# Mixture-of-experts stages with weigh-and-add from the accumulators, in a Trainium2 kernel of two attentions and two expert stages

## The chip, the core and the metric

The kernel runs on one core of a Trainium2 chip. The core has five engines that run side by side: TensorE (PE in the profile, with its weight loads as PEld), VectorE (DVE), ScalarE (ACT), GpSimd (POOL) and SyncE (SP), which only issues transfers. They wait for each other through semaphores. Matmul results land in the accumulator memory (PSUM), eight banks of 512 fp32 columns by 128 partitions; everything else that is worked on lies in SBUF. The metric is device microseconds for one execution, as a median of several.

## What is computed

An input `x` of 4 x 512 tokens by 128 features goes through four stages, each of the form x + stage(layernorm(x)): an attention with two steps of test-time training of its inner weights, a mixture of experts, a block-causal attention with 16 heads, and the same mixture of experts again with the same weights. The mixture of experts is what the change touches:

```
x_flat = x.reshape(-1, d)                                   # 2048 tokens, d = 128
gates = softmax(x_flat @ Wg + bg)                           # 8 experts
topk_gates, topk_idx = top_k(gates, 2)
topk_gates = topk_gates / sum(topk_gates)
expert_out = einsum('nd,edo->neo', x_flat, We) + be         # all 8 experts, 128 outputs each
out = sum over the two chosen experts of expert_out * topk_gates
x = x + out
```

All eight experts are computed for every token, and each result is weighed with a weight `wt` that is zero for the six experts that weren't chosen.

## The kernel before

The tokens stand as 16 tiles of 128 (`NT` = 16), in four groups of four tiles (`BATCH`, `TPB`, `SEQ` = 512). The kernel runs as phases: `qkv_phase`, twice `gradient_phase` and `schulz_phase`, `query_phase`, then `moe_phase(0)`, `attention_phase` and `moe_phase(1)`. Within a phase each engine has an instruction list of its own, and `pipeline` (line 77) writes a software pipeline for an engine: each step has a lag in tiles, and the middle of it is a hardware loop over two tiles at a time. The order on an engine is what the list says; semaphores `s_...` tie the engines together.

fp32 products are made of two fp32r parts: a high part (`xh`) and the remainder (`xl`), and `mm3` (line 114) issues three matmuls, high by high, high by low and low by high, with its lines 117, 118 and 119 in the profile.

`moe_phase` (line 969) has two parts. **Logits and weights:** VectorE normalizes four tiles (`norm`, line 1143), TensorE transposes them into `psT` (line 1096), ScalarE copies the 512 columns to `xTs` (line 1047), GpSimd copies them again into `xnT` (line 1021), TensorE multiplies with `wg` in plain fp32 (line 1103, output of 8 partitions), ScalarE takes the result with the gate's bias added (line 1052), TensorE transposes it back in pieces of 8 x 128 (line 1109), VectorE takes it (line 1153). After the four groups VectorE runs a chain of small steps, each waiting for the one before it: softmax with ScalarE's exponential (line 1070), the best and the second-best expert (`best`, line 1168), and the weights `wt` (line 1183). TensorE transposes `wt` (line 1115), ScalarE and VectorE part it (lines 1076, 1192), and TensorE makes the biases of all tiles, four banks by three matmuls (line 1119), which VectorE adds to `x` (line 1197).

**Experts, tile by tile:** ScalarE makes `xh` (line 1061), GpSimd `xl` (line 1034), TensorE two banks of 512 columns with three matmuls each (line 1131, shown as lines 117 to 119, output `m_E_`). VectorE weighs experts 0 to 3 in one operation (`weigh`, line 1204), ScalarE experts 4 to 7 one by one (line 1083), both into `y`. Then the eight are added: GpSimd adds halves of 512 columns (`add_half`, line 1030), VectorE quarters of 256 (line 1212), eighths of 128 (line 1217), and the last sum to `x` (line 1222). In the first of the two stages VectorE also takes the layernorm statistics of the tile (line 176, `stats`). There are two pairs of banks for `m_E_` and two buffers for each of `y`, `z`, `z2`, `z3`.

The weights of these stages are loaded and parted long before: `load_later_weights` (line 585) issues the loads, `part_later_weights` (line 606) parts them on GpSimd in the second `schulz_phase`, before GpSimd's line 671.

Of the kernel before, what the change touches and what calls it, by code (L numbers as in the profile page):

```python
# [22 lines left out]
F32 = mybir.dt.float32  # L23
# [6 lines left out]
P = 128  # L30
# [91 lines left out]
class Kernel:  # L122
    def __init__(self, nc, ctx, args, out):
# [13 lines left out]
        self.wg, self.bg = sb("wg", [P, NE]), sb("bg", [NE, 1])  # L137
# [447 lines left out]
    def load_later_weights(self, sp):  # L585
# [7 lines left out]
            (self.bg[:, :], self.a["L0_ffn_bg"].rearrange("(n a) -> n a", a=1)),  # L593
# [12 lines left out]
    def part_later_weights(self, pool):  # L606
# [362 lines left out]
    def moe_phase(self, nth):  # L969
# [8 lines left out]
        s_xn, s_xT, s_xTs, s_keep, s_L, s_l = (sem(n) for n in ("xn", "xT", "xTs", "keep", "L", "l"))  # L978
        s_sh, s_e, s_c, s_wT, s_wTs, s_B, s_xb = (sem(n) for n in ("sh", "e", "c", "wT", "wTs", "B", "xb"))
        s_hi, s_lo, s_E, s_y, s_z, s_z2, s_z3, s_x, s_out = (sem(n) for n in ("hi", "lo", "E", "y", "z", "z2", "z3", "x", "out"))  # L980
        s_prio, s_w, s_lT, s_lTs = sem("prio"), sem("w"), sem("lT"), sem("lTs")
        ACT_E = 4
        with ExitStack() as c:
            sb = lambda n, s, d=F32: c.enter_context(nc.sbuf_tensor(f"m{nth}_{n}_", s, d))
            ps = lambda n, s, d=F32: c.enter_context(nc.psum_tensor(f"m{nth}_{n}_", s, d))
            weh, wel, wg, bg, beh, bel = self.weh, self.wel, self.wg, self.bg, self.beh, self.bel
            xn, xTs, xnT = sb("xn", [P, 2, TPB, P]), sb("xTs", [P, 2, SEQ]), sb("xnT", [P, TOK])
# [3 lines left out]
            lTs = sb("lTs", [NE, 2, SEQ])  # L991
            wTh, wTl = sb("wTh", [P, P], F32R), sb("wTl", [P, P], F32R)
            xh, xl = sb("xh", [P, 2, P], F32R), sb("xl", [P, 2, P], F32R)
            y, z, z2, z3 = sb("y", [P, 2, NE * P]), sb("z", [P, 2, 4 * P]), sb("z2", [P, 2, 2 * P]), sb("z3", [P, 2, P])
            psT, psL = ps("T", [P, 2, 512]), ps("L", [P, 2, 512])
            psE = ps("E", [P, 2, NE * P])
            block = c.enter_context(nc.Block())
            tile = lambda t: bass.ds(t.i * 2 + t.j, 1)
            FIRST = [Tile(0, j) for j in range(2)]
            later = lambda step: lambda t: None if t.number() in (0, 1) else step(t)  # L1000

            @block.sync
            def _(sp):
                if nth == 1:
                    dst = self.out.rearrange("b (t p) d -> p (b t) d", p=P)
                    for g in range(BATCH):
                        sp.wait_ge(s_x, (g + 1) * TPB + 2)
# [4 lines left out]
            def _(pool):  # L1012
# [642 lines left out]
```

## Time and profile before

| | us |
|---|---|
| median of 3 runs | 913.87 (912.15 to 914.26) |
| the profiled execution, own time | 913.51 |
| its span, first to last instruction | 911.7 |
| TensorE busy | 778.6 (85%) |
| VectorE busy | 600.5 (66%) |
| ScalarE busy | 420.7 (46%) |
| GpSimd busy | 376.6 (41%) |
| mean granted TensorE clock | 0.946 of 2.4 GHz |
| first mixture-of-experts stage | about 406 to 476 |
| second mixture-of-experts stage | about 842.6 to the end |

Busy time is from an instruction's start to its end as recorded, also where it stands still in between; on an engine one may start before the one ahead of it has ended, so the distance between starts can be shorter than a duration. The granted clock is 1.00 at 2.4 GHz and 0.50 at 1.2 GHz. All times of rows are microseconds from the start of the span, unless marked ns.

### The profile page before, as it was taken

What the parts mean: (1) busy time and instruction counts of PE and PEld (TensorE: products, weight loads), DVE (VectorE), ACT (ScalarE), POOL (GpSimd) and SP (SyncE); (2) the same over time, 40 slices, a digit from 0 to 9 for tenths busy, and PEclk for the clock granted to TensorE, in tenths of its full rate; (3) what the DMA queues carried; (4) which work ended last, traced back from release to release, by engine and by line L of the source; (5) the groups of instructions that cost most, each with busy time, mean ns of one, the idle gap of its engine ahead of it and who ended that gap; (6) DMA issues with size and microseconds to landing.
All of it is one profiled execution on the core that took longest, in us unless ns stands there. A gap on an engine that the chain in (4) does not pass through costs nothing. (4 is left out here: it accounts for less than half of the span.)

```text
span 911.7 us, 16940 instructions
## 1 busy us (share of the span) xinstructions
PE 778.6 (85%) x5464; PEld 594.6 (65%) x5464; DVE 600.5 (66%) x1621; ACT 420.7 (46%) x1190; POOL 376.6 (41%) x512
## 2 busy tenths in 40 slices
PE   3669999879999667968628999999999999998763
PEld 1249999758999656755315766777777777777442
DVE  3936665355655556766996767766676666664698
ACT  4743332433333223314534666565556555562453
POOL 4854443015445534204642443343334333332275
PEclk9979999989999978997987999999999999999798
DMA  3030000000000000000000000000000000000001
GB/s 99 1 128 1 0 0 1 1 0 1 1 0 0 1 0 1 1 1 0 0 0 1 2 1 2 2 1 2 2 1 1 2 1 1 2 1 2 1 12 35
DMA packets 9327, 7.00 MB, mean 8 GB/s; under 512 B 1456, under 2 KB 8880, under 8 KB 9136
## 3 DMA queue, kind: packets, MB, share of 16 engines
q1 hardware_dynamic: 9264, 6.18, 2.1%
q8 instruction: 37, 0.61, 0.3%
q14 instruction: 26, 0.21, 0.1%
HBM read 5.13 MB, written 1.05 MB: 7 GB/s over the span
## 5 line engine op out<-in xcount | busy, mean ns | idle before, releaser
L1356 POOL TENSOR_SCALAR t_p_<-t_p_,t_rinv_ 128x128 f32<-128x128 f32 (+3 forms) x256 | 132.5, 535 | 213.5 <-DVE t_rinv_ L1551 213.5
L1544 DVE CUSTOM_DVE_ANT_0 t_p_<-t_S_,t_mask_ 128x128 f32<-128x128 f32 (+3 forms) x256 | 112.8, 487 | 72.7 <-PE t_S_ L1443 69.2
L1386 ACT ACTIVATE t_p_<-t_p_,t_nmin_ 128x128 f32<-128x128 f32 (+3 forms) x256 | 140.0, 551 | 9.0 <-DVE t_nmin_ L1544 9.0
L1391 ACT ACTIVATE t_pT_<-t_T_ 128x384 f32<-128x384 f32 (+1 forms) x96 | 50.7, 528 | 128.3 <-PE t_T_ L1455 128.3
L1455 PEld LDWEIGHTS t_T_<-ident,t_p_ 128*128 128x128 f32 x640 | 68.3, 140 | 44.6 <-POOL t_p_ L1356 28.7
L1443 PE MATMUL t_S_<-t_k_,t_q_ 64*128 64x256 f32 (+3 forms) x512 | 95.0, 469 | 0.0
L1470 PE MATMUL t_O_<-t_pT_,t_v_ 128*64 128x128 f32 x1280 | 91.0, 280 | 0.1
L1455 PE MATMUL t_T_<-ident,t_p_ 128*128 128x128 f32 x640 | 91.0, 281 | 0.0
L1470 PEld LDWEIGHTS t_O_<-t_pT_,t_v_ 128*64 128x64 f32 x1280 | 67.9, 136 | 29.9 <-ACT t_pT_ L1391 26.5
L432 POOL TENSOR_TENSOR g_sp<-g_s,g_t 128x512 f32<-128x512 f32 x32 | 40.9, 1277 | 103.3 <-DVE g_t L553 103.3
L1555 DVE COPY t_pT_<-t_T_ 128x384 f32<-128x384 f32 (+1 forms) x96 | 57.3, 597 | 3.1 <-PE t_T_ L1455 3.0
L544 DVE TENSOR_TENSOR g_sw<-g_G,g_s 128x512 f32<-128x512 f32 x32 | 22.1, 692 | 55.3 <-ACT g_s L456 55.3
L1030 POOL TENSOR_TENSOR m_z_<-m_y_ 128x512 f32<-128x512 f32 x32 | 43.4, 1355 | 27.9 <-DVE m_y_ L1204 27.9
L117 PE MATMUL m_E_<-weh,m_xh_ 128*128 128x512 f32 x64 | 29.2, 456 | 29.5 <-issue 14.9
L1443 PEld LDWEIGHTS t_S_<-t_k_,t_q_ 64*128 64x128 f32 x512 | 41.3, 185 | 18.9 <-issue 15.8
L1386 ACT ACTIVATION_READ_ACCUMULATOR t_p_<-t_p_,t_nmin_ 128x1 f32 x256 | 48.7, 190 | 0.0
L465 ACT ACTIVATE g_hT<-g_H 128x512 f32<-128x512 f32 x32 | 19.1, 597 | 58.3 <-PE g_H L497 58.3
L438 POOL TENSOR_TENSOR g_w<-g_u,g_sp 128x512 f32<-128x512 f32 x32 | 41.3, 1292 | 3.6 <-POOL g_sp L432 2.2
L1217 DVE TENSOR_TENSOR m_z_<-m_z_ 128x128 f32<-128x128 f32 x32 | 39.6, 1238 | 0.8 <-DVE x L1222 0.5
L117 PEld LDWEIGHTS m_E_<-weh,m_xh_ 128*128 128x128 f32 x64 | 13.0, 204 | 41.3 <-POOL m_xl_ L1034 19.9
L1083 ACT ACTIVATE m_y_<-m_E_,m_wt_ 128x128 f32<-128x128 f32 x128 | 36.4, 368 | 6.0 <-PE m_E_ L119 6.0
L504 PEld LDWEIGHTS g_PT<-proj,g_hT 128*128 128x128 f32 x256 | 33.6, 192 | 2.6
(270 smaller groups left out, 1849.4 us busy)
## 6 DMA issues: line engine op xcount, KB each, us to landing
wqkv<-in_L_attn_b_w_qkv_dram SPq DMA_DIRECT2D x1, 1536.0 KB
x<-in_L_attn_a_x_dram SPq DMA_DIRECT2D x4, 256.0 KB, 4.0
out_dram<-x SPq DMA_DIRECT2D x4, 256.0 KB, 2.3
we<-in_L_ffn_We_dram SPq DMA_DIRECT2D x1, 512.0 KB
wout<-in_L_attn_b_w_out_dram SPq DMA_DIRECT2D x1, 512.0 KB
proj<-n_L_attn_a_ttt_proj_dram SPq DMA_DIRECT2D x1, 256.0 KB, 6.1
gv<-n_L_attn_a_ttt_gate_dram SPq DMA_DIRECT2D x1, 256.0 KB, 5.1
gv<-in_L_attn_a_ttt_val_dram SPq DMA_DIRECT2D x1, 256.0 KB, 5.7
```

Of the source, the lines that this page charges most:

```text
L117: e.matmul(out, ah, bh, start=start, stop=False)
L432: pool.tensor_tensor(sp_[:, t.ring, :], s_[:, t.ring, :], t1[:, t.ring, :], ALU.subtract).then_inc(g["sp"], 1)
L438: pool.tensor_tensor(w1[:, t.ring, :], u_[:, t.ring, :], sp_[:, t.ring, :], ALU.mult).then_inc(g["w1"], 1)
L1030: pool.tensor_tensor(z[:, t.ring, :], y[:, t.ring, 0:4 * P], y[:, t.ring, 4 * P:8 * P], ALU.add).then_inc(s_z, 1)
L1356: last = pool.tensor_scalar(pr[:, G.par, h, cols], pr[:, G.par, h, cols], rinv[:, G.par, n:n + 1], 1.0, ALU.mult, ALU.mult)
L1386: act.activation(pr[:, G.par, h, cols], pr[:, G.par, h, cols], ACT.Exp, bias=nmin[:, G.par, n:n + 1], scale=-1.0, accum_out=rsum[:, G.par, ...
L1391: act.activation(pT[:, G.par, 0, G.blocks], psT[:, 0, 0:G.width], ACT.Copy).then_inc(t["eA"], 1)
L1443: last = pe.matmul(psS[:, (2 * G.n + h) % 3, at_:at_ + (qt + 1) * P], qp[d, G.par, qt * P:qt * P + P], kp[d, G.par, 0:(qt + 1) * P], start ...
L1455: last = pe.transpose(psT[:, h, k:k + P], pr[:, G.par, h, at_:at_ + P], ident[:, :])
L1470: last = pe.matmul(psO[d, qt * P:qt * P + P], v[:, G.b % 2, n, G.p * P + h * DH:G.p * P + h * DH + DH], pT[:, G.par, h, at_:at_ + P], star ...
L1544: dve.tensor_tensor_reduce(pr[:, G.par, h, cols], psS[:, (2 * G.n + h) % 3, at_:at_ + keys], mask[:, SEQ - keys:SEQ], 1.0, -NEG, ALU.add, ...
L1555: dve.tensor_copy(pT[:, G.par, 1, G.blocks], psT[:, 1, 0:G.width]).then_inc(t["eB"], 1)
```

## The change

Both mixture-of-experts stages are rewritten; the attentions are left as they are.

- The normalized and transposed tiles are parted straight from the bank: ScalarE writes `xh`, VectorE `xl`, for all 2048 tokens, once. Logits are `mm3` products with `xh` and `xl` of a tile as the stationary operand and the parted gate weights (`wgh`, `wgl`, 8 columns) as the moving one; they land with tokens on partitions. The gate's bias is added on VectorE. The softmax's division is left out, since the two chosen weights are divided by their sum anyway.
- TensorE makes tiles 0 and 1, then the biases, then the other tiles. The banks are a ring of four pairs. Tiles 2 and 3 use the four banks of the biases and wait until VectorE has added them.
- VectorE no longer weighs into `y`. It does five steps per tile (`take`): bank times weight plus running sum, for experts 0, 2 into `a` (beginning with `x`) and 1, 3, 4 into `b` (beginning with `z`). The steps of one turn belong to two tiles, in the order 1, 0, 3, 2, 4, so that each depends on the one two before it.
- ScalarE weighs experts 5 to 7 into `y`; GpSimd adds these three to `z` in two operations, and closes each tile with x = a + b.
- The loops are written out, with no hardware loop.

```diff
-        self.wg, self.bg = sb("wg", [P, NE]), sb("bg", [NE, 1])
+        self.wg, self.bg = sb("wg", [P, NE]), sb("bg", [P, 1, NE])
+        self.wgh, self.wgl = sb("wgh", [P, NE], F32R), sb("wgl", [P, NE], F32R)
...
+        c(pool.tensor_tensor(self.wgh[:, :], self.wg[:, :], self.ones[:, 0:NE], ALU.mult))
+        c(pool.tensor_tensor(self.wgl[:, :], self.wg[:, :], self.wgh[:, :].bitcast(F32), ALU.subtract))
...
+            def experts_of(t, first, count=1):
+                at = (4, 6, 0, 2)[t % 4] + first * P // 512
+                return psAll[:, at, first * P % 512:first * P % 512 + count * P]
+
+            def sums(t, e):
+                turn = t + LATER[e]
+                here = [k for k in ORDER if 0 <= turn - LATER[k] < NT]
+                return (ON_DVE * turn - 3 if turn else 0) + here.index(e) + 1
...
-                def add_half(t):
-                    pool.wait_ge(s_y, t.done() + 2)
-                    pool.wait_ge(s_w, t.done() + 2)
-                    pool.wait_ge(s_z2, t.done())
-                    pool.tensor_tensor(z[:, t.ring, :], y[:, t.ring, 0:4 * P], y[:, t.ring, 4 * P:8 * P], ALU.add).then_inc(s_z, 1)
+                def close(t):
+                    pool.wait_ge(s_a, sums(t, 4))
+                    pool.tensor_tensor(x[:, t, :], a[:, t % 4, :], b[:, t % 4, :], ALU.add).then_inc(s_x, 1)
+
+                for t in range(NT):
+                    r = t % 4
+                    if t > 1:
+                        close(t - 2)
+                    pool.wait_ge(s_y, t + 1)
+                    if t > 3:
+                        pool.wait_ge(s_a, sums(t - 4, 1))
+                    pool.tensor_tensor(z[:, r, :], y[:, r, 0:P], y[:, r, P:2 * P], ALU.add).then_inc(s_z, 1)
+                    pool.wait_ge(s_z, 2 * t + 1)
+                    pool.tensor_tensor(z[:, r, :], z[:, r, :], y[:, r, 2 * P:3 * P], ALU.add).then_inc(s_z, 1)
...
+                for g in range(BATCH):
+                    act.wait_ge(s_xT, g + 1)
+                    act.activation(xh[:, block_of(g)], psT[:, g % 2, :], ACT.Copy).then_inc(s_xh, 1)
...
+                def logits(g):
+                    pe.wait_ge(s_xl, g + 1)
+                    for t in range(g * TPB, (g + 1) * TPB):
+                        last = mm3(pe, psL[:, 0, t * NE:t * NE + NE], xh[:, tile_of(t)], xl[:, tile_of(t)], wgh[:, :], wgl[:, :])
...
                 def experts(t):
-                    pe.wait_ge(s_lo, t.done())
-                    pe.wait_ge(s_y, t.done())
-                    pe.wait_ge(s_w, t.done())
+                    if t > 3:
+                        pe.wait_ge(s_y, t - 3)
+                        pe.wait_ge(s_a, sums(t - 4, 4))
+                    elif t > 1:
+                        pe.wait_ge(s_xb, BATCH)
...
+                def low(g):
+                    dve.wait_ge(s_xh, g + 1)
+                    dve.tensor_tensor(xl[:, block_of(g)], psT[:, g % 2, :], xh[:, block_of(g)].bitcast(F32),
+                                      ALU.subtract).then_inc(s_xl, 1)
...
-                g(dve.tensor_reduce(tot[:, :], gate[:, :, :], AX.X, ALU.add))
-                g(dve.reciprocal(rtot[:, :], tot[:, :]))
-                g(dve.tensor_tensor(gate[:, :, :], gate[:, :, :], wide(rtot), ALU.mult))
...
+                for n, bank in enumerate(banks):
+                    rows = x[:, n * TPB:(n + 1) * TPB, :].rearrange("p t d -> p (t d)")
+                    dve.wait_ge(s_B, n + 1)
+                    dve.tensor_tensor(rows, bank, rows, ALU.add).then_inc(s_xb, 1)
...
+                def take(t, e):
+                    if e == 0:
+                        dve.wait_ge(s_E, t + 1)
+                        dve.wait_ge(s_xb, t // TPB + 1)
+                        if t > 3:
+                            dve.wait_ge(s_x, t - 3)
+                    if e == 1:
+                        dve.wait_ge(s_z, 2 * t + 2)
+                    if e > 1:
+                        dve.wait_ge(s_a, sums(t, (0, 1, 3)[e - 2]))
+                    acc = (a, b)[LATER[e]][:, t % 4, :]
+                    so_far = (x[:, t, :], z[:, t % 4, :])[e] if e < 2 else acc
+                    dve.scalar_tensor_tensor(acc, experts_of(t, e), weight(t, e), so_far, ALU.mult, ALU.add).then_inc(s_a, 1)
+
+                for t in range(NT + 1):
+                    for e in ORDER:
+                        if 0 <= t - LATER[e] < NT:
+                            take(t - LATER[e], e)
+                    if nth == 0 and t > 3:
+                        stats(t - 4)
```

## Rows read from the trace of the kernel before

**Rows 1.** Stretches: us, busy (x count) of PE, PEld, DVE, ACT, POOL, clock, DMA share.

```profile
872.00:900.00 28.00, 17.24 (x65) 10.91 (x63) 28.00 (x42) 14.06 (x52) 19.46 (x22) 1.00 0.06 19
```

**Rows 2.** Timeline of the second stage's loop: start, us, engine, line, what, [idle before].

```profile
884.33 1.40 POOL L1030 TENSOR_TENSOR m_z_<-m_y_ 128x512 f32<-128x512 f32 x1 [0.83 <-DVE m_y_ L1204]
884.35 0.47 PE L117 MATMUL m_E_<-weh,m_xh_ 128*128 128x512 f32 x1 [1.07 <-POOL m_xl_ L1034]
884.50 1.38 DVE L1217 TENSOR_TENSOR m_z_<-m_z_ 128x128 f32<-128x128 f32 x1
886.27 0.68 DVE L1204 TENSOR_TENSOR m_y_<-m_E_,m_wt_ 128x512 f32<-128x512 f32 x1
...
900.54 0.47 PE L117 MATMUL m_E_<-weh,m_xh_ 128*128 128x512 f32 x1 [1.07 <-POOL m_xl_ L1034]
```

**Rows 3.** Timeline of VectorE: weights and end, first stage; end, second stage.

```profile
426.69 0.29 DVE L1183 TENSOR_TENSOR m_wt_<-m_sel_,m_rtot_ 128x128 f32<-128x128 f32 x1
...
474.82 0.48 DVE L176 BATCH_NORM_STATS2 stats<-x 128x6 f32<-128x128 f32 x2
...
908.51 0.49 DVE L1222 TENSOR_TENSOR x<-x,m_z_ 128x128 f32<-128x128 f32 x2
```

**Rows 4.** Timeline around the bias matmuls, second stage.

```profile
863.17 0.29 DVE L1183 TENSOR_TENSOR m_wt_<-m_sel_,m_rtot_ 128x128 f32<-128x128 f32 x1
...
864.69 0.50 PE L117 MATMUL m_T_<-beh,m_wTh_ 128*128 128x512 f32 x1 [0.76 <-DVE m_wTl_ L1192]
...
865.26 0.40 PE L119 MATMUL m_T_<-beh,m_wTl_ 128*128 128x512 f32 x1
...
867.36 0.40 PE L119 MATMUL m_T_<-beh,m_wTl_ 128*128 128x512 f32 x1
...
867.57 1.28 POOL L1030 TENSOR_TENSOR m_z_<-m_y_ 128x512 f32<-128x512 f32 x1
...
867.80 0.69 DVE L1197 TENSOR_TENSOR x<-m_T_,x 128x512 f32<-128x512 f32 x1 [1.96 <-PE m_T_ L119]
```

**Rows 5.** Groups by line and shape: what xcount | busy us, mean ns | idle before.

```profile
L839 DVE SCALAR_TENSOR_TENSOR gv<-acc,n_rate,gv 128x512 f32<-128x512 f32 x4 | 3.0, 751 | 3.1 <-PE acc L738 2.9
...
L822 DVE COPY n_A<-n_small 128x128 f32<-128x128 f32 x18 | 5.0, 280 | 0.0
...
L800 DVE TENSOR_SCALAR n_A<-n_small,n_r 128x128 f32<-128x128 f32 x12 | 3.8, 348 | 15.7 <-PE n_small L678 15.6
...
L1034 POOL TENSOR_TENSOR m_xl_<-m_xnT_,m_xh_ 128x128 fp32r<-128x128 f32 x32 | 15.5, 488 | 20.4 <-ACT m_xh_ L1061 20.4
...
L438 POOL TENSOR_TENSOR g_w<-g_u,g_sp 128x512 f32<-128x512 f32 x32 | 41.3, 1292 | 3.6 <-POOL g_sp L432 2.2
```

**Rows 6.** Timeline of VectorE, end of the first stage's loop.

```profile
467.13 0.28 DVE L1222 TENSOR_TENSOR x<-x,m_z_ 128x128 f32 x1
467.33 0.28 DVE L176 BATCH_NORM_STATS2 stats<-x  x1
```

**Rows 7.** Timeline of the second stage's logits.

```profile
847.17 0.60 ACT L1047 ACTIVATE m_xTs_<-m_T_ 128x512 f32<-128x512 f32 x1 [3.05 <-PE m_T_ L1096]
...
851.51 0.32 PEld L1109 LDWEIGHTS m_E_<-ident,m_lTs_ 8*128 8x128 f32 x4 [0.86 <-ACT m_lTs_ L1052]
...
855.97 0.19 DVE L1153 COPY m_logit_<-m_E_ 128x32 f32<-128x32 f32 x1 [0.65 <-PE m_E_ L1109]
...
856.52 0.29 DVE L1161 TENSOR_TENSOR m_logit_<-m_logit_,m_m_ 128x128 f32<-128x128 f32 x1
...
857.20 0.29 ACT L1070 ACTIVATE m_gate_<-m_logit_ 128x128 f32<-128x128 f32 x1
```

**Rows 8.** Stretches of one us before and at the bias matmuls.

```profile
857.00:858.00 1.00, 0.27 (x1) 0.30 (x2) 0.44 (x2) 0.49 (x3) 0.83 (x2) 0.50 0.00 0
...
864.00:865.00 1.00, 0.31 (x1) 0.30 (x2) 0.65 (x2) 0.96 (x4) 0.21 (x1) 1.00 0.00 0
```

**Rows 9.** Timeline of GpSimd in the second Schulz phase.

```profile
352.66 2.49 POOL L671 TENSOR_TENSOR gvl<-gv,gvh 128x512 fp32r<-128x512 f32 x2 [24.92 <-ACT gvh L776]
```

More of the change, by code:

```diff
@@ L1078, in weigh_last @@
-                def weigh_last(t):
-                    act.wait_ge(s_E, t.done() + 2)
-                    act.wait_ge(s_z, t.done())
-                    for n in range(NE - ACT_E, NE):
-                        cols = slice(n * P, n * P + P)
-                        last = act.activation(y[:, t.ring, cols], psE[:, t.ring, cols], ACT.Copy,
-                                              scale=wt[:, tile(t), n:n + 1].rearrange("p a e -> p (a e)"))
-                    last.then_inc(s_w, 1)
-                pipeline(act, (0, later(high)), (1, weights_high), (2, weigh_last))()
+                act.wait_ge(s_wT, 1)
@@ new lines, in _ @@
+                act.activation(wTh[:, :], psT[:, 0, 0:P], ACT.Copy).then_inc(s_wh, 1)
+                for t in range(NT):
+                    act.wait_ge(s_E, t + 1)
+                    if t > 3:
+                        act.wait_ge(s_z, 2 * t - 6)
+                    for k in range(NE - ON_DVE):
+                        e = ON_DVE + k
+                        last = act.activation(y[:, t % 4, tile_of(k)], experts_of(t, e), ACT.Copy, scale=weight(t, e))
+                    last.then_inc(s_y, 1)
@@ L1089, in _, with turn @@
             @block.tensor
             def _(pe):
-                def turn(t):
-                    pe.wait_ge(s_xn, t.done())
-                    if t.number() not in (0, 1):
-                        pe.wait_ge(s_xTs, t.done(-1))
+                def turn(g):
+                    pe.wait_ge(s_xn, g + 1)
+                    if g > 1:
+                        pe.wait_ge(s_xl, g - 1)
                     for n in range(TPB):
-                        last = pe.transpose(psT[:, t.ring, n * P:n * P + P], xn[:, t.ring, n, :], ident[:, :])
+                        last = pe.transpose(psT[:, g % 2, tile_of(n)], xn[:, g % 2, n, :], ident[:, :])
@@ L1097, in turn @@
                     last.then_inc(s_xT, 1)
                 def logits(g):
-                    pe.wait_ge(s_xTs, g.done())
-                    pe.wait_ge(s_lTs, g.done())
-                    pe.matmul(psL[0:NE, g.ring, :], wg[:, :], xTs[:, g.ring, :], start=True, stop=True).then_inc(s_lT, 1)
-                def turn_logits(g):
-                    pe.wait_ge(s_lTs, g.done() + 2)
-                    pe.wait_ge(s_l, g.done())
-                    for n in range(TPB):
-                        last = pe.transpose(psE[:, g.ring, n * NE:n * NE + NE], lTs[:, g.ring, n * P:n * P + P], ident[0:NE, 0:NE])
-                    last.then_inc(s_L, 1)
@@ L1136, in _ @@
+                turn(0)
+                for g in range(BATCH):
+                    if g + 1 < BATCH:
+                        turn(g + 1)
+                    logits(g)
+                experts(0)
+                experts(1)
+                biases()
+                for t in range(2, NT):
+                    experts(t)
             @block.vector
             def _(dve):
-                n = self.ln_vector(dve, s_var, s_root, s_ln)
-                dve.sem_inc(s_xT, 2)
-                dve.sem_inc(s_l, 2)
@@ L1219, in add_x @@
-                def add_x(t):
-                    dve.wait_ge(s_z3, t.done() + 2)
-                    dve.wait_ge(s_xb, 1)
-                    dve.tensor_tensor(x[:, tile(t), :], x[:, tile(t), :], z3[:, t.ring, :], ALU.add).then_inc(s_x, 1)
-                def stats(t):
-                    dve.wait_ge(s_x, t.done() + 2)
-                    self.take_stats(dve, t.i * 2 + t.j)
-                last = ((6, stats),) if nth == 0 else ()
-                pipeline(dve, (2, weigh), (1, add_bias), (3, add_quarter), (4, add_eighth), (5, add_x), *last)()
+                dve.wait_ge(s_wh, 1)
@@ L1231, in moe_phase @@
+                for t in range(NT + 1):
[4 more added lines that the diff above has]
+                        stats(t - 4)
+                if nth == 0:
+                    for t in range(NT - 3, NT):
+                        stats(t)
         if nth == 0:
```

185 lines of the change are left out of this document (62 added, 123 removed).

## The prediction

> **What bounds the kernel now.** The page comes first: no engine is busy throughout, and 85% for TensorE is a mean over stages. So I read the two mixture-of-experts stages by themselves. In a stretch of the second one's loop the table of stretches has VectorE busy all the time at 28.00 of 28 us, TensorE 17.24, GpSimd 19.46, ScalarE 14.06 [rows 1]. But VectorE's busy time is not work: in the timeline of one tile its 128x128 add of line 1217 takes 1.38 us, beginning as GpSimd's 1.40 us add of line 1030 runs and ending with it, where an operation of its shape elsewhere takes 0.28 [rows 2, 6]. It stands still beside GpSimd. The circle is: VectorE weighs (0.68), GpSimd adds the half (1.40), VectorE's next adds come free only then, VectorE weighs again. TensorE's tile comes every (900.54 - 884.35) / 6 = 2.70 us [rows 2], though its six matmuls need 6 x 0.233 = 1.40 us: between the line 119 rows at 865.26 and 867.36 lie nine steps, 0.233 each [rows 4]. So the loop is bound by the VectorE-GpSimd circle, not by an engine's work.
>
> I count both stages from C, the end of the weights `wt` (line 1183). Second stage: C = 863.17 + 0.29 = 863.46, last `x` at 909.00, so C + 45.5. First stage: C = 426.98, the last statistics at 475.30, so C + 48.3 [rows 3, 4].
>
> **Costs of the new steps.** A take is a VectorE scalar_tensor_tensor of 128x128 from a bank, with a per-partition scalar and a second operand in SBUF. The nearest row, line 839, is just this at 128x512: 751 ns, against 685 for line 1197, an add from a bank without such a scalar [rows 4, 5]. At 128x128, line 800 has the scalar at 348 ns and line 822 has none at 280. So a take lasts some 0.35 us, of which about 0.07 is for the scalar. Start to start is shorter than a duration: in the first stage 128x128 operations lasting 0.28 begin 0.20 apart, each with its own wait [rows 6]. So a take costs 0.20 + 0.07 = 0.27 us, and five 1.35 us per tile; statistics in the first stage add 0.20. From below the take could cost 0.20 (5 x 0.20 = 1.00, and TensorE would bind), from above its full 0.35 (1.75). I take 0.27 because the 0.08 of overlap is in every pair I see. Waits on the accumulator reach two takes back (the order 1, 0, 3, 2, 4 sees to it), and 2 x 0.27 is over 0.35, so they should not hold.
>
> The Trainium skill (VectorE: DVE Perf Modes, "The DRAIN you can't avoid") says the next VectorE operation can't issue until the pipe is empty. Taken as full durations end to end, five takes would be 1.75 us; the 0.20 steps under 0.28 durations speak against that reading [rows 6], and the result it would give is the second rival below.
>
> GpSimd now does three 128x128 adds per tile (two of `z`, one closing into `x`). Line 1034 has this shape at 488 ns, and line 438, which waits for the add before it, idles 2.2 us over 32, about 0.07 each [rows 5]. Back to back I count 0.44 each, plus 0.07 for the one that waits: 1.39; ends 1.3 and 1.6. ScalarE has three weighings instead of four and no parting (lines 1061 and 1083 now, 14.06 of 28 us busy with both): about 0.9 us per tile, hidden. TensorE keeps 1.40. All three are near 1.4. GpSimd's turn begins when VectorE's turn ends, and VectorE needs its `z` a turn later: two turns hold 0.08 + 1.39 + 0.05 + 1.35 = 2.87, with 0.08 and 0.05 for the two hand-overs, near the 0.07 of line 438; so 1.44 per tile. I take T = 1.44 in the second stage and, with statistics, 1.35 + 0.20 = 1.55 in the first.
>
> **Prelude, up to C.** Now the logits are done at 855.97 + 0.19 = 856.16 [rows 7]. Removed: four copies on GpSimd, the 8-row transposes, line 1052's copies, all on this chain. Added: 16 x 3 matmuls with a 128-column stationary and 8 moving columns, and the parting of `x` in front of them. ScalarE's part is ready 847.17 + 0.60, VectorE's subtraction is 0.69: the first logits start at about 848.6. The nearest row is line 1109, 8x128 stationary, 8 columns: four loads span 0.32 us with the last one's own length, so they are at most 0.08 apart, at full clock, and 0.16 at half [rows 7]. I count the stretch as running at half, as its first part did before, and take 0.125: 48 x 0.125 = 6.0 us, plus two groups of transposes at about 1.0 each: 856.5, that is +0.4. Bounds: at full clock 48 x 0.08 = 3.8 or less, where the copy and subtraction of each group bind, about -1.0; with 8 rows being no guide to 128, up to 0.20 each, 48 x 0.20 + 2.0 + 848.6 = 860.2, +4.
>
> The Trainium skill (TensorE: Matmul & The Clock Gate, "LDWEIGHTS (loading the stationary operand)") says that a load's time goes by columns, not rows, about columns / 1.2 ns. By that an estimate is 107 ns each and 5.1 us for 48, inside my bounds.
>
> Behind the logits VectorE gains one chained step, the add of the gate's bias, and loses three, the sum, its reciprocal and the multiplication; at some 0.3 each (0.29 in the row of line 1183 and its wait) that is -0.6. The exponential starts at 857.20, though its input is there at 856.52 + 0.29, since it stands behind two `xh` copies on ScalarE [rows 7]; without them it starts some 0.3 earlier. Together -0.9. So C moves by +0.4 - 0.9 = -0.5 us, between -1.9 and +3.1.
>
> **From C to the end.** The transposition, two partings and the first bias matmul are unchanged: 864.69 = C + 1.23. The banks are ready at about C + 2.2, 2.9, 3.6 and 4.3 (the last, at 867.36 + 0.40). VectorE now adds each as it comes, 0.69 each: done at C + 5.05, where before it weighed two tiles first. But all takes stand behind these four adds on VectorE, and the third tile's matmuls wait for them too, since tiles 2 and 3 use the bias banks: ready 0.08 + 0.57 + 3 x 0.233 + 0.40 later, C + 6.8. Takes begin at C + 5.05; two (0.54) and then five (1.35) give C + 6.95, so this wait is just covered. After it turns step by T: turn 16 starts at C + 6.95 + 14 x 1.44 = C + 27.1. Its three takes (0.81 + 0.08), the hand-over (0.08) and the closing add (0.45) give C + 28.5, against C + 45.5: 17.0 us.
>
> First stage: turns 2 and 3 without statistics, twelve at 1.55: 6.95 + 2.88 + 18.6 = C + 28.4, the takes to C + 29.3, the closing add 29.8, the last statistics (0.28) C + 30.2 with hand-over, against 48.3: 18.1 us.
>
> Everything else is taken at nothing. The two added GpSimd splits of `wg` lie ahead of a 24.92 us idle time [rows 9]; without that cover they cost some 0.4 us. The broadcast load of `bg` goes through the same queue, in front of that idle time. Unrolling the loops adds instructions; the attention stage already runs unrolled. The output transfers follow `x` as before.
>
> Sum: 17.0 + 18.1 + 2 x 0.5 = 36.1. The profiled execution took 913.51 (span 911.70, 1.8 around it), the median is 913.87: 913.5 - 36.1 = 877.4.
>
> **Rivals.**
> Forecast, 876 +- 4: 0.60.
>
> First rival, the clock: 0.22. TensorE has a gap before the bias matmuls. Before, the granted clock is 0.50 (1.2 GHz) from 857 to 858, behind a gap, while the first two tiles' 12 matmuls begin, and 1.00 (2.4 GHz) from 864 to 865, after they ran, just as the bias matmuls begin [rows 8]. The logits now end in short bursts, the first two tiles follow at once, and then TensorE waits for C 2 to 4 us. If the bias matmuls run at 1.2 GHz, where 512 columns take 0.43 us, 12 x (0.43 - 0.233) = 2.4 us come in front of all takes, and up to 1 more for tile 2: 2.4 to 3.4 per stage, time 882 to 884.
>
> Second rival, takes cost their duration: 0.12. T = 1.75 and 1.95. Second stage: C + 5.05 + 7 x 0.35 + 14 x 1.75 + 1.6 = 33.6, +5.1. First: some +6.2. Time 889.
>
> Third, slower than before, GpSimd against the takes: 0.04. If a take, whose second operand is in SBUF, stands still beside GpSimd as line 1217 does, the two add up: 1.39 + 1.35 = 2.74, with the hand-overs 2.8, and 2.95 in the first stage. That is +19 and +20 on the forecast, 917. It decides from a turn of about 2.7. Against it: line 1197, one operand in a bank and one in SBUF, takes 0.69 at 867.80 while GpSimd's add runs from 867.57 to 868.85, and that add stays at 1.28 [rows 4].
>
> Fourth: the ring does not loosen the order, for instance since GpSimd's adds cost 0.55 each: T = 1.7, +3.6 and +1.8, 883; within the range, 0.02 by itself.
>
> Range: from 873 (prelude 1.4 shorter in both stages, T = 1.40) to 889, with little beyond it. Faster 0.95, within 0.3% 0.01, slower 0.04; 0.3% is about what a measurement of this kernel can tell from no change.
>
> **What would show it.** In the loop, takes of 0.35 us beginning 0.27 apart, whatever GpSimd does; TensorE's tiles 1.4 to 1.5 us apart at clock 1.00; the first take 5 us after `wt`; logits matmuls 0.06 to 0.12 apart. The prediction is wrong if takes stretch beside GpSimd, if the clock shows 0.50 between C and C + 7, or if the logits take over 8 us.

## The result, and the profile after

| | before | after |
|---|---|---|
| median, us | 914.07 (4 runs, 912.15 to 914.3) | 888.63 (4 runs, 885.27 to 890.14) |
| profiled execution, own time | 913.51 | 889.06 |
| its span | 911.7 | 887.3 |
| mean granted clock | 0.946 | 0.934 |
| first expert stage, from its first layernorm step to the next stage's | 406.07 to 476.21, 70.14 | 405.42 to 462.68, 57.26 |
| second, to the end | 842.65 to 911.7, 69.05 | 829.02 to 887.3, 58.28 |

The changed kernel takes 0.9721 of the time of before [0.969, 0.9752], 2.8% less. It is faster, as forecast, and 888.6 lies inside the range of 873 to 889, but at its slow end: the forecast was 877.4. The two stages lost 12.9 and 10.8 us where 18.6 and 17.5 were expected (the stretch up to the next stage included). Everything else moved by 0.75 us in all (0.65 ahead of the first stage).

I put the two executions side by side at four marks per stage: the first layernorm step, C (the end of `wt`), the first take, the end of the last take. Between marks, in us:

| | forecast, stages 1 / 2 | after | off by |
|---|---|---|---|
| layernorm step to C (before: 20.91 / 20.81) | 20.4 / 20.3 | 23.97 / 23.83 | +3.6 / +3.5 |
| C to first take | 5.05 / 5.05 | 7.34 / 7.35 | +2.3 / +2.3 |
| first take to end of last | 24.2 / 22.9 | 24.2 / 23.8 | 0.0 / +0.9 |

So the loops came out nearly as forecast in sum, and two pieces ahead of them, the logits and the bias matmuls, cost 11.7 us more. The lines show why.

**The loop.** Timeline of the changed kernel, second stage (start, us, engine, line, what, [idle before]); line 1187 is the take, 1043 and 1045 GpSimd's two additions to `z`, 1034 the closing add.

```profile
865.39 0.35 DVE L1187 SCALAR_TENSOR_TENSOR m_b_<-m_A_,m_wt_,m_z_ 128x128 f32<-128x128 f32 x1
...
866.45 0.46 POOL L1045 TENSOR_TENSOR m_z_<-m_z_,m_y_ 128x128 f32<-128x128 f32 x1
...
866.86 0.46 POOL L1034 TENSOR_TENSOR x<-m_a_,m_b_ 128x128 f32<-128x128 f32 x1
866.94 0.35 DVE L1187 SCALAR_TENSOR_TENSOR m_b_<-m_A_,m_wt_,m_z_ 128x128 f32<-128x128 f32 x1 [0.17 <-POOL m_z_ L1045]
...
867.21 0.34 DVE L1187 SCALAR_TENSOR_TENSOR m_a_<-m_A_,m_wt_,x 128x128 f32<-128x128 f32 x1
867.28 0.46 POOL L1043 TENSOR_TENSOR m_z_<-m_y_ 128x128 f32<-128x128 f32 x1
...
867.47 0.34 DVE L1187 SCALAR_TENSOR_TENSOR m_b_<-m_A_,m_wt_,m_b_ 128x128 f32<-128x128 f32 x1
...
868.32 0.35 DVE L1187 SCALAR_TENSOR_TENSOR m_b_<-m_A_,m_wt_,m_z_ 128x128 f32<-128x128 f32 x1
...
882.91 0.35 DVE L1187 SCALAR_TENSOR_TENSOR m_b_<-m_A_,m_wt_,m_z_ 128x128 f32<-128x128 f32 x1
```

A take lasts 0.34 to 0.35 and the next begins 0.26 later, while GpSimd adds beside it: compare [rows 2], where VectorE's add beside GpSimd's took 1.38. Turns alternate between 1.38 (866.94 to 868.32) and 1.55 (865.39 to 866.94), the longer one with 0.17 of waiting for GpSimd's `z`; two turns take 2.93, forecast 2.87. From the fourth turn (its first take at 864.02) to the seventeenth, 882.91, a turn is 18.89 / 13 = 1.45.

**The logits.** Timeline of the changed kernel's second stage: 128 columns of `xh` or `xl` as the stationary operand, which is loaded before each matmul, and 8 columns of gate weights as the moving one.

```profile
834.72 0.35 PE L118 MATMUL m_A_<-wgl,m_xh_ 128*128 128x8 f32 x1
...
834.93 0.35 PE L119 MATMUL m_A_<-wgh,m_xl_ 128*128 128x8 f32 x1
...
835.14 0.35 PE L117 MATMUL m_A_<-wgh,m_xh_ 128*128 128x8 f32 x1
```

They are 0.21 apart; I had 0.125. They begin at 834.48 and TensorE turns to the first tile at 846.28: 11.8 us, where my sum has 8.0.

**The clock.** Stretches of the changed kernel, second stage: from:to, us, busy (x count) of PE, PEld, DVE, ACT, POOL, granted clock, DMA share.

```profile
831.00:832.00 1.00, 0.00 (x0) 0.00 (x0) 1.00 (x5) 0.00 (x0) 0.00 (x0) 1.00 0.00 0
...
833.00:834.00 1.00, 0.95 (x5) 0.72 (x4) 0.33 (x2) 0.60 (x1) 0.00 (x0) 0.50 0.00 0
...
835.00:849.00 14.00, 14.00 (x62) 13.42 (x62) 5.38 (x16) 2.79 (x4) 0.00 (x0) 0.50 0.00 0
...
850.00:851.00 1.00, 0.71 (x4) 0.23 (x2) 0.90 (x4) 0.00 (x0) 0.00 (x0) 1.00 0.00 0
...
853.00:854.00 1.00, 0.38 (x1) 0.08 (x1) 0.28 (x1) 0.59 (x3) 0.00 (x0) 0.50 0.00 0
...
858.00:859.00 1.00, 1.00 (x4) 0.66 (x2) 0.69 (x1) 0.00 (x0) 0.00 (x0) 0.50 0.00 0
...
861.00:882.00 21.00, 19.25 (x83) 14.67 (x81) 19.59 (x72) 12.40 (x42) 17.75 (x41) 1.00 0.13 38
```

The whole of the logits ran at 1.2 GHz, though TensorE is busy for 14.00 of 14 us (the logits up to 846.28, then tile 0). The clock came to 1.00 in the course of the matmuls of tiles 0 and 1, stayed there through most of the idle time behind them, and was at 0.50 again when the biases began.

**From C to the first take.** Timeline of the changed kernel: end of the weights, their transposition, first bias matmuls, VectorE's first and last bias addition (line 1169), first take.

```profile
852.56 0.29 DVE L1163 TENSOR_TENSOR m_wt_<-m_sel_,m_rtot_ 128x128 f32<-128x128 f32 x1
...
852.90 0.47 PE L1099 MATMUL m_A_<-ident,m_wt_ 128*128 128x128 f32 x1 [2.19 <-DVE m_wt_ L1163]
...
854.66 0.63 PE L118 MATMUL m_A_<-bel,m_wTh_ 128*128 128x512 f32 x1
...
855.09 0.63 PE L119 MATMUL m_A_<-beh,m_wTl_ 128*128 128x512 f32 x1
...
855.75 0.69 DVE L1169 TENSOR_TENSOR x<-m_A_,x 128x512 f32<-128x512 f32 x1 [1.74 <-PE m_A_ L119]
...
859.59 0.69 DVE L1169 TENSOR_TENSOR x<-m_A_,x 128x512 f32<-128x512 f32 x1 [0.59 <-PE m_A_ L119]
860.20 0.34 DVE L1187 SCALAR_TENSOR_TENSOR m_a_<-m_A_,m_wt_,x 128x128 f32<-128x128 f32 x1
```

TensorE idles 2.19 before the transposition; then bias matmuls stand 0.43 apart against 0.233 in [rows 4], and VectorE waits 0.59 before each bank but the first. That is the first rival. In the kernel before, the clock was not high all along either: the two tiles' matmuls ran at 0.50 to their end, and it rose only then. Its timeline and two of its stretches, lines that I had not taken:

```profile
862.55 0.63 PE L119 MATMUL m_E_<-weh,m_xl_ 128*128 128x512 f32 x1
863.52 0.42 PE L1115 MATMUL m_T_<-ident,m_wt_ 128*128 128x128 f32 x1 [0.34 <-DVE m_wt_ L1183]
```

```profile
862.00:863.00 1.00, 1.00 (x3) 0.36 (x2) 0.87 (x4) 0.00 (x0) 0.00 (x0) 0.50 0.00 0
863.00:864.00 1.00, 0.60 (x2) 0.18 (x1) 0.43 (x2) 0.00 (x0) 0.00 (x0) 0.62 0.00 0
```

There the two tiles' matmuls had begun late and ended only 0.34 ahead of the transposition; the clock rose between 863 and 864 and was 1.00 at the bias matmuls [rows 8]. In the changed kernel they end 2.19 ahead of it.

### The profile page after: what moved, and what is told of

Read it like the earlier page. It is cut to its first block and busy times, and to the rows that moved or that the text cites. A ratio compares the mean times of both kernels' runs of the same rounds, so it can differ in the third digit from the quotient of the medians.

```text
span 887.3 us, 16341 instructions
## 1 busy us (share of the span) xinstructions
PE 785.5 (89%) x5510; PEld 615.7 (69%) x5512; DVE 564.9 (64%) x1649; ACT 400.4 (45%) x1118; POOL 351.9 (40%) x538
## 5 line engine op out<-in xcount | busy, mean ns | idle before, releaser
L1066 ACT ACTIVATE m_y_<-m_A_,m_wt_ 128x128 f32<-128x128 f32 x96 | 28.1, 368 | 27.3 <-PE m_A_ L119 27.3
L1043 POOL TENSOR_TENSOR m_z_<-m_y_ 128x128 f32<-128x128 f32 x32 | 14.8, 461 | 50.8 <-ACT m_y_ L1066 50.8
L524 PE MATMUL acc<-qkv,g_dg 128*128 (+1 forms) x256 | 34.0, 276 | 1.0 <-DVE g_dg L572 1.0
L505 PE MATMUL g_PT<-proj,g_hT 128*128 128x128 f32 x256 | 34.1, 276 | 0.0
L524 PE MATMUL acc<-qkv,g_du 128*128 (+1 forms) x256 | 33.8, 275 | 0.0
```

What stands on the lines that cost most here:

```text
L505: last = pe.matmul(pred, hT[:, t.ring, n * P:n * P + P], self.proj[:, n, :], start=(n == 0), stop=(n == NC - 1))
L524: last = pe.matmul(self.acc[:, n, m, :], src[:, t.ring, m * P:m * P + P], d[:, t.ring, :] if n == 2 else k, start=False, stop=False, skip_ ...
```

## The experiments

Two questions were open: what the logits and the biases cost and why, and whether GpSimd plays a part in the takes. Two numbers from each trace serve below: from the layernorm step to C, and from C to the first take, stage 1 / stage 2 (changed kernel: 23.97 / 23.83 and 7.34 / 7.35). The untouched phases ahead of the first stage end between 404.5 and 409.5 us over these executions (405.4 in the changed kernel's), so single spans don't compare within 5 us. Stretches between marks do: those that an edit leaves alone repeat within 0.4 in these profiles, of which there is one per kernel.

**Fill TensorE's gap before the biases.**

```diff
+def keep_busy(count):
+    for n in range(count):
+        pe.matmul(psL[:, 1, :], xh[:, 0:P], weh[:, 0:512], start=True, stop=True)
 def biases():
+    keep_busy(9)
     pe.wait_ge(s_c, 1)
...
+    keep_busy(2)
     pe.wait_ge(s_wl, 1)
```

> The changed kernel with matmuls that nobody reads put into TensorE's gap before the bias matmuls: nine of 512 columns behind the first two tiles, two more behind the transposition of the weights. The output is the reference's. My theory: the bias matmuls run at half clock only because TensorE stands idle for about 2.2 us in front of them. With the gap filled they begin at clock 1.00, the twelve take 0.23 us apart instead of 0.43, the first take comes about 5 us after the weights instead of 7.35, and the kernel is 2.3 us faster in each stage, 4 to 5 us in all. Rival: the clock at that point follows from what the engine did earlier, in the logits; then it is 0.50 there all the same and the kernel is the same or up to 1 us slower by the added matmuls.

Measured: 886.19 us, ratio 0.9691 [0.9662, 0.9721]. First take at C + 5.64 / 4.79. Stretches of this kernel, from the end of the filling to the loop:

```profile
853.00:855.00 2.00, 1.78 (x9) 1.02 (x8) 1.00 (x4) 0.79 (x4) 0.00 (x0) 1.00 0.00 0
855.00:859.00 4.00, 3.22 (x13) 2.33 (x14) 3.07 (x6) 1.03 (x4) 1.81 (x4) 1.00 0.00 0
```

With the gap filled the clock stays at 1.00 and the second stage's first take comes 2.56 earlier; in the first stage 1.70, where the filling itself held up the biases (their transposition began 0.98 behind C). So the half clock in the biases of the changed kernel comes from the gap and costs the 2.3 us that the table above has for it. The median fell by 2.4 only, where 4 to 5 were expected and the stretches' sum is 4.3; in the profiled execution the first stage began at 408.10, 2.7 later.

**Keep the clock up at the start of a stage.**

```diff
+for n in range(12):
+    pe.matmul(psL[:, 1, :], weh[:, 0:P], weh[:, 0:512], start=True, stop=True)
 turn(0)
```

> The changed kernel with twelve matmuls of 512 columns that nobody reads at the start of each mixture-of-experts stage, where TensorE waits for the layernorm. The output is the reference's. Theory A: a load with eight moving columns counts as work for the clock, so an engine that enters the logits at 1.00 stays there; the logits' matmuls are then 0.107 us apart instead of 0.213, the logits end 5 us earlier in each stage, and the kernel is 8 to 10 us faster. Theory B, which I hold: the loads don't keep the clock up (in the changed kernel TensorE was busy all the time from 835 to 846 at 0.50); the clock falls within the logits and at most some 1 to 3 us per stage are gained, if the start isn't delayed by the added matmuls.

Measured: 879.54 us, ratio 0.9641 [0.9599, 0.9683]; to C 21.36 / 20.20; first take at C + 4.78 / 6.23. Timeline of TensorE in this kernel, first logits, and stretches of it, two in the second stage's logits and two at the bias matmuls, of the first stage and at the end of those of the second:

```profile
829.63 0.25 PE L118 MATMUL m_A_<-wgl,m_xh_ 128*128 128x8 f32 x1
829.74 0.25 PE L119 MATMUL m_A_<-wgh,m_xl_ 128*128 128x8 f32 x1
```

```profile
829.00:832.00 3.00, 2.61 (x24) 2.51 (x23) 3.00 (x10) 1.05 (x2) 0.00 (x0) 1.00 0.00 0
...
834.00:842.00 8.00, 8.00 (x30) 7.13 (x30) 3.70 (x12) 1.50 (x2) 0.00 (x0) 0.50 0.01 2
...
427.00:432.00 5.00, 3.39 (x13) 2.31 (x13) 3.13 (x7) 1.82 (x7) 1.81 (x4) 1.00 0.00 0
...
849.00:851.00 2.00, 1.22 (x4) 0.42 (x2) 1.41 (x3) 0.00 (x0) 0.00 (x0) 0.69 0.00 0
```

At 2.4 GHz these matmuls are 0.11 apart, so their price follows TensorE's clock. But the clock didn't last, as theory B had it: it fell to 0.50 at 833 to 834 with TensorE occupied throughout and no gap. Small matmuls, each with a load of its own, neither raised the clock (changed kernel) nor held it (here).

The gain is larger than theory B's 1 to 3 us per stage. 2.6 and 3.6 us of it lie before C, and 2.6 and 1.1, which no theory had, behind it: tiles 0 and 1 end nearer to C, and TensorE idles 1.15 and 1.16 ahead of the transposition instead of 2.10 and 2.19. In the first stage all bias matmuls then run at 1.00. In the second, behind the same idle time, they begin at 1.00, 0.23 apart, and from 846.94 stand 0.43 apart. So the length of the idle time alone doesn't tell the clock behind it.

**Fewer loads.** High and low gate weights side by side, 16 moving columns, so that two matmuls per tile replace three; VectorE adds the two halves.

```diff
-last = mm3(pe, psL[:, 0, t * NE:t * NE + NE], xh[:, tile_of(t)], xl[:, tile_of(t)], wgh[:, :], wgl[:, :])
+pe.matmul(psL[:, 0, t * 2 * NE:(t + 1) * 2 * NE], xh[:, tile_of(t)], self.wgs[:, :], start=True, stop=False)
+last = pe.matmul(psL[:, 0, t * 2 * NE:t * 2 * NE + NE], xl[:, tile_of(t)], wgh[:, :], start=False, stop=True)
```

> The changed kernel with the two parts of the gate weights side by side, so that the high part of a tile is the stationary operand once, with 16 moving columns, instead of twice with eight: 32 matmuls per stage instead of 48, and one more small step on VectorE. The output is the reference's. My theory: a matmul of the logits costs its load, whatever the moving columns: 0.213 us each at half clock, so 16 fewer save 3.4 us per stage, the added step costs 0.3, and the kernel is 6 us faster. Rival: the distance is set by the moving side or by issue; then 16 columns take longer each, and less than 2 us come out.

Measured: 881.92 us, ratio 0.9644 [0.9615, 0.9673]; to C 20.94 / 20.56; the first take stays at C + 7.21 / 7.36. Timeline of TensorE in this kernel, at clock 0.50:

```profile
836.29 0.36 PE L1083 MATMUL m_A_<-wgs,m_xh_ 128*128 128x16 f32 x1
836.50 0.35 PE L1084 MATMUL m_A_<-wgs,m_xl_ 128*128 128x8 f32 x1
836.71 0.36 PE L1083 MATMUL m_A_<-wgs,m_xh_ 128*128 128x16 f32 x1
```

Sixteen moving columns cost what eight do, 0.21: what is paid is the matmul with its load, whatever moves. Sixteen of them less gave 3.0 and 3.3 us; 16 x 0.213 is 3.4, less the added VectorE step. A price of the load and a fixed price of every matmul aren't told apart by this run; line 1109's loads, at most 0.08 apart at full clock [rows 7] against 0.11 here, speak against a fixed one of that size.

**The logits turned round.** Gate weights stationary, 512 tokens moving, as before the change, but in fp32r parts and with the copy and transposition back. With this TensorE transposes one group of `x` further ahead of the logits, and waits for VectorE's subtraction of the maximum before tile 1; the rest is as in the changed kernel.

```diff
-for t in range(g * TPB, (g + 1) * TPB):
-    last = mm3(pe, psL[:, 0, t * NE:t * NE + NE], xh[:, tile_of(t)], xl[:, tile_of(t)], wgh[:, :], wgl[:, :])
+mm3(pe, psL[0:NE, g % 2, :], wgh[:, :], wgl[:, :], xh[:, block_of(g)], xl[:, block_of(g)]).then_inc(s_lT, 1)
...
+last = pe.transpose(psAll[:, 7, at:at + NE], lTs[:, g % 2, tile_of(n)], ident[0:NE, 0:NE])
```

> The changed kernel with the logits the way round that the kernel before had: the gate weights (8 columns) are the stationary operand, four tiles (512 columns) move, three matmuls per group instead of twelve; ScalarE takes the 8 x 512 result and TensorE transposes it back in four pieces per group. The expert loop is as in the changed kernel, the output the reference's. My theory: twelve loads at 0.213 us per group (2.6) give way to three streams of 0.43 (1.3) and small transposes, the logits end about 3 to 4 us earlier per stage; the streams may also raise the clock earlier. 6 to 8 us faster in all, unless a longer gap before the bias matmuls gives some of it back. Rival: the chain through ScalarE and back costs what the loads cost; the same within 2 us.

Measured: 879.97 us, ratio 0.9625 [0.9593, 0.9657]; to C 18.69 / 20.09; first take at C + 6.32 / 7.36. Stretches and timeline of this kernel's second stage:

```profile
826.00:832.00 6.00, 4.34 (x16) 2.73 (x17) 5.15 (x18) 1.78 (x3) 0.00 (x0) 0.59 0.00 0
833.00:840.00 7.00, 6.28 (x37) 4.13 (x37) 2.66 (x8) 3.95 (x6) 0.00 (x0) 0.94 0.00 0
...
844.00:845.00 1.00, 0.48 (x1) 0.18 (x1) 0.29 (x1) 0.14 (x1) 0.00 (x0) 0.55 0.00 0
```

```profile
834.55 0.39 PE L118 MATMUL m_A_<-m_xl_,wgh 128*8 128x512 f32 x1
834.78 0.40 PE L119 MATMUL m_A_<-m_xh_,wgl 128*8 128x512 f32 x1
```

Three streams of 512 columns do four tiles in 1.28 us at half clock and 0.70 at full, where twelve loads took 2.56. And among them the clock rose (0.94 in 833 to 840) where among the small matmuls it had not, with TensorE busy for less of the time (6.28 of 7). So C comes 5.3 and 3.7 earlier. What is given back is the bias: tiles 0 and 1 now end at full clock and the gap before C grows to 3.5. In the second stage the first take is again at C + 7.36. In the first stage, behind 3.52 of idle time, the first bias matmuls still stand 0.22 to 0.34 apart, and only from 427.89, while TensorE works, 0.43; the first take comes at C + 6.32. The layout that the change had removed is better than its three loads per tile.

**The closing add on VectorE.** Both of its operands lie in SBUF, as line 1217's did.

```diff
-def close(t):
-    pool.wait_ge(s_a, sums(t, 4))
-    pool.tensor_tensor(x[:, t, :], a[:, t % 4, :], b[:, t % 4, :], ALU.add).then_inc(s_x, 1)
...
+def close(t):
+    dve.wait_ge(s_a, sums(t, 4))
+    dve.tensor_tensor(x[:, t, :], a[:, t % 4, :], b[:, t % 4, :], ALU.add).then_inc(s_x, 1)
...
+if e == 0 and t > 1:
+    close(t - 2)
```

> The changed kernel with the closing add x = a + b moved from GpSimd to VectorE, two turns after its tile; GpSimd keeps the two adds of z. The output is the reference's. The add has both operands in SBUF, as line 1217 of the kernel before had, while a take has one in a bank. Theory: an SBUF-to-SBUF add on VectorE stands still while GpSimd adds, so its 0.28 us are stretched, up to GpSimd's 0.46 and more, a turn goes from 1.46 to 1.6 to 1.9, and the kernel is 4 to 13 us slower; takes stay at 0.34. Rival: the standstill of line 1217 had another cause; then the add costs its 0.20 to 0.28, a turn stays at 1.5 to 1.6 and GpSimd is relieved, within 2 us of the changed kernel.

Measured: 894.15 us (2 runs), ratio 0.9759 [0.9714, 0.9805], whose interval overlaps the changed kernel's. The marks decide: from the first take to the end of the last it is 27.1 / 25.4 against 24.2 / 23.8, 2.9 and 1.6 longer; a turn takes 1.69 / 1.57 against 1.49 / 1.45. Timeline of this kernel (line 1183 is the add), and its group over 860 to 892 beside that of a take (what xcount, busy us, mean ns, idle before):

```profile
869.66 0.46 POOL L1037 TENSOR_TENSOR m_z_<-m_y_ 128x128 f32<-128x128 f32 x1 [0.38 <-ACT m_y_ L1058]
...
869.84 0.42 DVE L1183 TENSOR_TENSOR x<-m_a_,m_b_ 128x128 f32<-128x128 f32 x1
...
871.48 0.28 DVE L1183 TENSOR_TENSOR x<-m_a_,m_b_ 128x128 f32<-128x128 f32 x1
...
872.95 0.63 POOL L1039 TENSOR_TENSOR m_z_<-m_z_,m_y_ 128x128 f32<-128x128 f32 x1
```

```profile
L1183 DVE TENSOR_TENSOR x<-m_a_,m_b_ 128x128 f32<-128x128 f32 x16 | 5.4, 340 | 0.0
L1179 DVE SCALAR_TENSOR_TENSOR m_a_<-m_A_,m_wt_,x 128x128 f32<-128x128 f32 x16 | 5.4, 337 | 0.0
```

The add that starts inside GpSimd's ends 0.14 behind GpSimd's end (870.26 and 870.12), as line 1217's in [rows 2] ended 0.15 behind. Another, started at 872.98, is untouched, and GpSimd's own operation is 0.63 instead of 0.46, though its recorded start is 0.03 earlier. So either can be the one that waits, and when the starts are that close the records don't tell which it will be. The takes stay at 0.34: of VectorE's operations only the one with both inputs in SBUF is hit. The Trainium skill (SBUF — State Buffer, "SBUF: two separate sides") states this as an exclusive lock on a shared pair of ports, held for the whole of an instruction by whichever starts first; the rows agree with it, but for the order at 872.95, and with its exception for an operand outside SBUF.

So the mechanism is the theory's, but its price is near the rival's: of 16 adds 5 in the second stage and 2 in the first are stretched, by 0.14 to 0.21, some 1.0 and 0.3 us in all. The larger part of the 1.6 and 2.9 is a sixth operation, 0.20 per turn, on an engine that was nearly full. A reason for the low price may be that GpSimd's operation is 0.46 long here and not 1.40; no run varies that.

**One GpSimd addition less.** Expert 7 is left out of the sum.

```diff
 pool.wait_ge(s_z, 2 * t + 1)
-pool.tensor_tensor(z[:, r, :], z[:, r, :], y[:, r, 2 * P:3 * P], ALU.add).then_inc(s_z, 1)
+pool.sem_inc(s_z, 1)
```

> The changed kernel without GpSimd's second add of z, so expert 7 is left out of the sum; everything else is done. Theory: in the second stage GpSimd's three adds, 1.45 us, bind the turn, with VectorE waiting some 0.1 to 0.2 for z each turn; with two adds the turn falls to TensorE's 1.37 and VectorE's wait for z goes, about 1.2 us in the second stage. In the first stage VectorE binds with its statistics at 1.49, and the turn stays there. Rival: the turn is bound by VectorE's takes in both stages, and stays at 1.45 and 1.49.

Measured: 885.91 us, one run. From the first take to the end of the last 23.65 / 22.31, so 1.5 less in the second stage and 0.6 in the first; 0.5 of each is the fourth turn, which starts 1.40 behind the third instead of 1.88. Timeline of VectorE in this kernel, first take of each turn:

```profile
868.75 0.35 DVE L1187 SCALAR_TENSOR_TENSOR m_b_<-m_A_,m_wt_,m_z_ 128x128 f32<-128x128 f32 x1
...
870.12 0.35 DVE L1187 SCALAR_TENSOR_TENSOR m_b_<-m_A_,m_wt_,m_z_ 128x128 f32<-128x128 f32 x1
```

Turns are 1.37 now, which is TensorE's 6 x 0.229. So in the second stage it is GpSimd's hand-over that makes 1.45 of 1.37; in the first, VectorE with its statistics binds, and the turn stays at 1.48.

**Together.** The turned logits, or the shared load, each with the matmuls at the start of the stage and the filling (14 and 2, or 10 and 2).

> Three of the changes put together: logits turned as in the kernel before, twelve unread matmuls at the start of a stage, and unread matmuls (fourteen and two) in front of the bias matmuls. The output is the reference's. If the terms add, the weights come 18 to 19 us after the stage's first step (23.9 in the changed kernel) and the first take 4.8 us after them (7.35), some 7 to 8 us per stage: 872 to 876 us. Rival: the terms share the same microseconds, since the clock that the streams of the logits give is the clock that the unread matmuls give; then it ends at 878 or above, hardly better than either alone.

> As the run before, but with the logits made of two matmuls per tile, a load of the high part with 16 moving columns and one of the low part with eight. The output is the reference's. Loads of 0.11 us at full clock and 0.21 at half: if the clock falls within the logits as it did with the unread matmuls alone, the weights come about 18 us after the stage's first step and the kernel ends at 873 to 878; if the shorter logits are over before the clock falls, up to 2 us better. Rival: loads lower the clock sooner, and it ends above 879.

Measured: 875.53 us (872.95 to 876.85), ratio 0.9552 [0.9516, 0.9589], and 875.01 (874.62 to 875.65), ratio 0.9552 [0.952, 0.9583]. To C 19.62 / 18.34 and 19.65 / 19.65; first take at C + 5.82 / 4.78 and 4.81 / 4.77. Stretches of the first of the two, second stage:

```profile
830.00:840.00 10.00, 9.30 (x51) 6.31 (x51) 6.22 (x20) 4.55 (x7) 0.00 (x0) 1.00 0.01 2
841.00:845.00 4.00, 3.44 (x15) 2.29 (x14) 2.18 (x5) 1.83 (x7) 1.70 (x4) 1.00 0.00 0
```

These are 4.5% below before and 1.7% below the changed kernel by the two ratios (0.9552 / 0.9721). That the medians are near the 877.4 forecast for the changed kernel is chance: they hold unread matmuls and other logits.

Both times lie where they were expected, but the terms don't add. Alone, the turned logits, the matmuls at the start and the filling gave 8.7, 9.1 and 2.4 us by the medians; in one kernel they give 13.1. What the filling gives is kept: the clock is 1.00 from C to the first take. But to C the turned logits needed 18.69 / 20.09 without the matmuls at the start and 19.62 / 18.34 with them, 0.8 less in sum, where these matmuls alone had given 6.2; here the rival, that both give the same clock, is nearly borne out. With the shared load they still give 2.2 (41.5 to 39.3 in sum), but C comes at 19.65 and not at the expected 18, and the clock fell within the logits again (0.50 from 829 on in the second stage). In the first stage of the turned kernel the fourteen filling matmuls were too many: the transposition began 1.17 behind C.

## Why the prediction was right, and where it was not

By the prediction's own signs three came out against it: the clock shows 0.50 between C and C + 7, the logits take 11.8 us and not up to 8, and their matmuls are 0.21 apart and not 0.06 to 0.12. The signs in the loop came out for it. That 888.6 still lies inside the range is in part luck: its end of 889 was the price of takes at full duration, which didn't occur, and the two misses that did, 7.1 for the logits and 4.6 for the clock, would end at 877.4 + 11.7 = 889.1 if nothing else had moved.

**What bounds the kernel: right, as far as is shown.** In the loop of before VectorE stood beside GpSimd; a take reads one operand from a bank, none is stretched, and the turn went from 2.70 to 1.45. The change also took operations from both engines and loosened the ring, and no run separates these parts.

**The loop: right within 0.9 us, in the first stage by two errors against each other.** A take was put at 0.35 and 0.27 apart, measured 0.34 and 0.26; GpSimd's adds at 0.44 apart, measured 0.42; the turn at 1.44 and 1.55, measured 1.45 and 1.49. The second rival, takes at their full duration, is refuted by the 0.26. By it, the reading of the Trainium skill's rule (VectorE: DVE Perf Modes, "The DRAIN you can't avoid") that no operation starts before the pipe is empty doesn't hold for takes; the same section says that a next operation that is not held starts earlier. The third, takes that stand still beside GpSimd, is refuted by the loop's rows, and the closing-add run shows that the mechanism was real. That the operand in the bank spared the takes, and not their kind of operation, rests on line 1197, an add of the closing add's kind with one operand in a bank, which stayed at 0.69 beside GpSimd [rows 4]. The fourth failed too, with 0.46 for an add. Of the 0.9 us missing in the second stage, 0.4 is a step that I called "just covered": the third tile waits for the bias banks, its `z` comes late, and turn 3 starts 1.88 behind turn 2 (862.14 to 864.02) instead of 1.44. Another 0.2 is the end of the last turn, and 0.2 is 13 turns at 0.01 more. The first stage has the same late turn (1.89) and end, 0.7 us together, and its turns of 1.48 to 1.49 instead of 1.55 give 0.7 back, hence the 0.0.

**The prelude: the term for the logits was mis-sized.** I took 0.125 us for each of 48 matmuls, from line 1109 in [rows 7], whose stationary operand is 8 x 128 in plain fp32 and whose loads are 0.08 apart at most. Measured: 0.213 at half clock, 10.2 us instead of 6.0. I counted the stretch as running at half clock, where I had 0.16 by this row, and still took less. My bound of 0.20, kept because 8 rows might be no guide to 128, put C 3.1 later, and 3.0 came. So the value was chosen by the nearest row in name, and the bound, which had no row of its own, was near the answer. The Trainium skill's rule for the load (TensorE: Matmul & The Clock Gate, "LDWEIGHTS (loading the stationary operand)"), some 107 ns for 128 columns, fits the 0.111 between these matmuls at full clock; at half clock it is twice that, which the rule doesn't say and my estimate of 5.1 us left out. By its other half, that rows make no difference, line 1109 with its 128 columns should have been a guide, and at 0.08 or less against 0.111 it was not; the type differs too (plain fp32), and no run here varies one alone.

**The clock: the first rival took place, with 2.3 of its 2.4 to 3.4 us, in both stages.** I had the mechanism and gave it 0.22. The step of the sum that failed is the price of the bias matmuls: the first began at C + 1.22, as forecast, but the twelve were put at 0.233 each, with the banks ready by C + 4.3, and stood 0.43 apart. What spoke for the rival was in the trace: the two tiles' matmuls of before ended 0.34 us ahead of the transposition, and the change makes that gap longer whatever the logits cost, since those matmuls then begin directly behind the logits. I read in [rows 8] that the clock was 1.00 at the bias matmuls and didn't ask how long TensorE had been idle. Filling the gap confirmed it.

Sum: 3.6 + 3.5 for the logits, 2 x 2.3 for the clock, 0.9 in the second loop, less 0.75 in the untouched phases: 11.85, against 36.1 - 24.4 = 11.7; the rest is rounding and 0.07 behind the last takes of the first stage.

**Not settled.** Why TensorE's clock falls under loads with few moving columns: the runs show that it does, not what the chip counts. When it falls behind idle time: the first stage of the turned logits kept 1.00 over 3.52 us and lost it later, the changed kernel lost it within 2.19. Nor why the untouched phases differ by up to 5 us between these kernels.

## What to carry to other kernels

An operation that reads one operand from an accumulator bank runs beside GpSimd at its full speed; one that reads both from SBUF can wait for it, or hold it up, so weigh-and-add straight from the bank is worth more than its saved instruction. When a product has one narrow side, try the narrow side as the stationary one: here a load of 128 columns was paid in full for 8 moving columns. And for any matmuls behind a wait, look up in the trace how long TensorE has been idle before them, and if the change makes that idle time longer, carry a second sum with them at half clock; how much of it comes true varied between the stages of one run.

## What the hardware showed that I had not expected

- TensorE busy for 14.00 of 14 us kept a granted clock of 0.50 when its work was, for the first 11 of them, 128-column loads with 8 moving columns, and in another run the clock fell from 1.00 to 0.50 in the middle of such work; a stretch with 512-column streams, busy for 6.28 of 7 us, had 0.94.
- The clock was 0.50 behind 2.19 us of idle time between the first tiles and the biases, and 1.00 behind 0.34 of it in the kernel before. Behind 1.15 and 1.16, in two stages of one run, it stayed at 1.00 once and fell in the middle of the bias matmuls once; behind 3.52 it was still 1.00 and fell within 2 us of the end of it.
- An unread matmul can pay for itself: 12 of them at the start of each expert stage made the kernel 7 to 9 us faster (ratios to before 0.9721 and 0.9641, medians 888.6 and 879.5).
- A collision between VectorE and GpSimd can fall on either: 0.42 instead of 0.28 on VectorE, 0.63 instead of 0.46 on GpSimd.
